# A two-layer transformer kernel on one core: scalings and copies moved to ScalarE, five element-wise steps to GpSimd, tanh products in pairs, and a new order of the work

## The chip, the core and the metric

The program runs on one core of a Trainium2 chip. The core's engines run their own instruction queues side by side: TensorE (PE; its weight loads are listed as PEld), VectorE (DVE), ScalarE (ACT), GpSimd (POOL) and SyncE (SP), which here only issues DMAs. An engine executes its queue strictly in order; between engines, work is ordered by semaphores. The metric is the device time of one execution in microseconds (us), the median of several runs.

## The reference, cut to what matters

Input: `hidden_states` of shape (8, 256, 128): 8 sequences of 256 tokens with 128 features, all in float32. Four blocks, each with a residual and a layer norm in front:

```python
x = x + L0_attn(layernorm(x))   # 16 heads of 8, softmax, relative positions (rel_k, rel_v, clipped at 20)
x = x + L0_ffn(layernorm(x))    # per token: softmax attention between its 16 heads, then 8 experts mixed by a softmax gate
x = x + L1_attn(layernorm(x))   # linear attention by a second-order Taylor expansion, 8 heads of 16
x = x + L1_ffn(layernorm(x))    # top-2 of 8 experts + a shared one: silu((x@w1+b1)*(x@w3+b3)) @ w2 + b2
```

The silu is computed with a tanh: `h * (1 + tanh(h))` on halved values.

## The kernel before

One sequence ("image" t, 0 to 7) is the unit. Its 256 tokens lie as 2 blocks (`C = 2`) of 128 partitions. The work of one image is cut into 141 small *pieces* (`norm0`, `scores` 0 to 7, `turn` 0 to 15, `dot` 0 to 3, `chunk` 0 to 14, `join` 0 to 4 and so on), in five lists: PREPARE (first layer norm, q/k/v), ATTENTION (the softmax attention), FEED (attention between heads, gate, experts), SECOND (Taylor attention), LATE (routing, hidden chunks, expert sum, store).

**The order.** Each piece has a position, a whole number written by hand in `PREPARE_AT`, `ATTENTION_AT`, `FEED_AT`, `SECOND_AT` and `LATE_AT` (L83 to L108). Piece k of image t stands at `t * PERIOD + position`, with `PERIOD = 480`. Every engine walks through all pieces sorted by this number (`turns`, L329) and issues what it has to do in each. So four to five images are in work at a time: beside the attention of image t each engine does the FEED of t-1, the SECOND of t-2 and the LATE of t-2 and t-3. The 8 `scores` pieces stand at 0, 60, 120 ... 420. In this text *slot k* is the stretch of positions from 60k up to 60(k+1), taken modulo 480; each slot begins with the piece `scores` k. No position is a time: it only fixes the order in the queues.

**What the pieces that matter do.**
- `scores` k: 32 matmuls on PE (L1026, L1036) into two PSUM banks, a maximum on DVE (L725), an exponential on ACT (L451). PE may start `scores` k+1 only when the exponential of k is done. `turn` transposes the weights (L1047; evicted by ACT, L459), `relative` multiplies them with the table of relative values (L1065, L1068). After the last ones `keep_rv` 3 (ACT, L435) lets SP write `rvs` to DRAM (L373, 8 DMAs) and read it back as `relo` (L376, L378); `divide` (DVE, L731 to L739) needs it.
- `moments` (DVE, L678): a layer norm's mean and variance: 2 `bn_stats` and 6 small instructions that combine the halves. `normed` (DVE, L695): the scaling, one instruction a block. GpSimd takes the -0.5th power (L544, L579, L595, L606).
- `dot`, `dot_sum`, `soft`, `soft_sum`, `mix`, `mix_sum`, `mix_scale` (FEED, nearly all DVE, L768 to L813): the attention between heads of a token: 4 products and 4 sums of 1024 elements a partition, a softmax over 512 elements, again 4 products and 4 sums.
- `chunk` n (LATE): two matmuls of 256 columns (L1224, L1225), an addition on ACT (L516), a product on DVE (L934: u), tanh on ACT (L521), and a second product on DVE (L939: hidden). 13 chunks an image. All but the last two images use one PSUM bank for them, the last two use two.
- `join` n: the experts' output matmuls (L1245 to L1254), added up by DVE (L947, L953) in the same bank, so `join` n+1 on PE waits for the DVE part of `join` n.
- `rank` (DVE, L904 to L927): the top-2 choice, twelve small steps one after another. `divide3` (DVE, L872 to L886), `qkv3` with the copy of v (DVE, L870), `scale2` (DVE, L825), `split0` (DVE, L712) whose result goes out by DMA and comes back as `qc` for GpSimd's `blocks` (L545 to L559), which `scores` 0 and 4 need.

## Time and profile before

| | |
|---|---|
| median of 3 runs | 813.42 us (812.59 to 817.56) |
| the profiled execution | 821.41 us, its span 819.6 us |
| busy in the span | PE 671.8, PEld 532.3, DVE 567.0, ACT 393.2, POOL 153.0 us |
| mean granted TensorE clock | 0.937 (1.00 from about 265 to 683 us) |

The span runs from the first to the last instruction. Each engine's busy time is the sum of its instructions' spans with overlaps counted once. The TensorE clock is given as a share of full speed. The profile names the instruction by engine, line and operands; "x8" is a count of instructions; a float32 matmul or transpose shows as one or two instructions, depending on the operation. "Idle before, releaser" is the engine's idle time ahead of an instruction and what ended it.

### The profile page before, as it was taken

Reading aid. Unit: us, or ns where it says so; the run is one execution under the profiler, and the core shown is the slowest. Engines: PE = TensorE matmul, PEld = TensorE weight load, DVE = VectorE, ACT = ScalarE, POOL = GpSimd, SP = SyncE. Lnnn points to the kernel's source line nnn. Section 1 sums busy time; section 2 is a strip of 40 time slices with the busy share of each in tenths; the row PEclk is TensorE's granted clock in tenths of the full one; section 3 lists DMA queues with packets and bytes.
Section 4 is the critical chain, followed back from the end, with each engine's and each line's share of the span. In section 5 each row is a group of like instructions: output and inputs, shape, how many; then the busy total and the mean of one; then the engine's idle time right before and its main releaser. Section 6 shows DMA issues by size and latency. Waiting matters only on the chain.

```text
span 819.6 us, 16984 instructions
## 1 busy us (share of the span) xinstructions
PE 671.8 (82%) x6432; PEld 532.3 (65%) x6432; DVE 567.0 (69%) x1482; ACT 393.2 (48%) x953; POOL 153.0 (19%) x179
## 2 busy tenths in 40 slices
PE   2377772887799899989998999889998995877886
PEld 1256651775587678767886688668876773656655
DVE  3122178458876997699769985998589857787174
ACT  1164333544565556555556555665565453324241
POOL 2311120412040205030403041202221102011000
...
DMA packets 75958, 13.45 MB, mean 16 GB/s; under 512 B 69851, under 2 KB 74981, under 8 KB 75749
## 3 DMA queue, kind: packets, MB, share of 16 engines
...
q0 software_dynamic: 384, 1.05, 0.4%
q10 hardware_dynamic: 180, 0.48, 0.2%
...
## 4 chain that ended last, share of the span: by engine, by line
PE 39%; issue 34%; DVE 12%; ACT 6%; POOL 3%; SPq 3%; DMA 2%; POOLq 0%; ACTq 0%
PE bank L1026 5%; PE bank L1047 4%; PE bank L1224 4%; PE bank L1065 3%; PE bank L1225 3%; PE bank L1145 3%; DVE nmx L725 2%; PE bank L1089 2%; PE bank L1036 2%; ACT pm L451 2%; POOL q3h L602 2%; PE bank L1178 1%; SPq L373 1%; SPq L349 1%; PE bank L965 1%
## 5 line engine op out<-in xcount | busy, mean ns | idle before, releaser
L451 ACT ACTIVATE pm<-bank,nmx 128x256 f32<-128x256 f32 x256 | 100.5, 475 | 126.3 <-DVE nmx L725 126.3
L725 DVE TENSOR_REDUCE nmx<-bank 128x2 f32<-128x512 f32 x128 | 82.3, 684 | 72.7 <-PE bank L1036 72.6
L1047 PE MATMUL bank<-w,pm 128*128 128x128 f32 x512 | 84.5, 291 | 29.6 <-ACT pT L459 24.4
L1026 PE MATMUL bank<-kT,qbd 64*64 64x256 f32 x1024 | 90.7, 417 | 13.2 <-issue 12.9
L459 ACT ACTIVATE pT<-bank 128x512 f32<-128x512 f32 x128 | 77.2, 603 | 38.1 <-PE bank L1047 37.9
L1047 PEld LDWEIGHTS bank<-w,pm 128*128 128x128 f32 x512 | 63.7, 151 | 42.7 <-ACT pm L451 30.5
L934 DVE SCALAR_TENSOR_TENSOR hu<-bank,w,ha 128x256 f32<-128x256 f32 x104 | 50.1, 482 | 53.3 <-ACT ha L516 52.9
L1065 PE MATMUL bank<-tv,pT 128*128 128x128 f32 (+1 forms) x512 | 84.7, 284 | 0.0
L1065 PEld LDWEIGHTS bank<-tv,pT 128*128 128x128 f32 x512 | 75.0, 202 | 3.5 <-issue 2.1
L516 ACT ACTIVATE ha<-bank,w 128x256 f32<-128x256 f32 x104 | 49.7, 478 | 55.1 <-PE bank L1225 54.2
L1224 PE MATMUL bank<-xfT,w 128*128 128x256 f32 x208 | 66.6, 402 | 8.5 <-DVE hu L934 8.5
L1225 PE MATMUL bank<-xfT,w 128*128 128x256 f32 x208 | 62.5, 382 | 0.0
L1036 PE MATMUL bank<-tkw,qr 64*64 64x96 f32 (+1 forms) x1024 | 56.4, 269 | 0.0
L1036 PEld LDWEIGHTS bank<-tkw,qr 64*64 64x64 f32 x1024 | 47.5, 143 | 13.5 <-issue 2.5
L501 ACT ACTIVATE sq<-bank,half_root 128x512 f32<-128x512 f32 x64 | 40.9, 698 | 29.7 <-PE bank L1178 29.7
L1178 PE MATMUL bank<-q3h,k 64*128 64x256 f32 x256 | 40.1, 434 | 13.5 <-ACT sq L501 10.7
L1026 PEld LDWEIGHTS bank<-kT,qbd 64*64 64x64 f32 x1024 | 33.4, 142 | 25.8 <-issue 23.2
L521 ACT ACTIVATE ht<-hu 128x256 f32<-128x256 f32 x104 | 43.1, 414 | 7.0 <-DVE hu L939 6.3
L939 DVE SCALAR_TENSOR_TENSOR hu<-ht,hu 128x256 f32<-128x256 f32 x104 | 45.9, 448 | 0.4 <-ACT ht L521 0.4
L557 POOL TENSOR_TENSOR qr<-qc,half_mask 128x512 f32<-128x512 f32 x32 | 33.5, 1068 | 67.3 <-DMA qc<-d_qdh 67.3
L606 POOL TENSOR_TENSOR rs_c<-ve_c,expo 128x2 f32<-128x2 f32 x8 | 5.6, 700 | 211.7 <-DVE ve_c L693 211.7
L853 DVE SCALAR_TENSOR_TENSOR x<-bank,gl,x 128x128 f32<-128x128 f32 x128 | 35.9, 343 | 12.6 <-PE bank L1145 12.5
...
## 6 DMA issues: line engine op xcount, KB each, us to landing
...
```

Of the source, the lines that this page charges most:

```text
L451: a = act.activation(pm[:, s % 2, c, j], b_s[c][:, j * S:(j + 1) * S], exp, bias=nmx[:, i:i + 1])
L459: act.activation(view(pT, (c * RTC + 2 * s) * C * P, [[1, 2 * C * P]]), b_t[:], copy).then_inc(pT_ready[0], 1)
L516: act.activation(ha[:, n % 2], late_bank(t, n)[:, 0:S], idn, scale=0.5, bias=wc("b1", n, n + 1)).then_inc(a_ready[0], 1)
L725: v.tensor_reduce(nmx[:, i:i + 2], b_s[c][:].rearrange("p (j k) -> p j k", j=2), AX_X, ALU.max, negate=True).then_inc(max_ready[0], 1)
L934: v.scalar_tensor_tensor(hu[:, n], late_bank(t, n)[:, S:2 * S], wc("b3", n, n + 1), ha[:, n % 2], ALU.add, ALU.mult).then_inc(u_ready[0], 1)
L1026: mm(b_s[c][cols:cols + P // 2, j * S:(j + 1) * S], qbd[rows:rows + P // 2, i], kT[rows:rows + P // 2, t % 2, u], start=True, stop=False, ...
L1036: a = mm(b_s[c][cols:cols + P // 2, j * S + lo:j * S + hi], qr[rows:rows + P // 2, i], tkw[rows:rows + P // 2, KB // QI - 1 - i % (KB // Q ...
L1047: a = nc.tensor.transpose(b_t[:, (j * 2 + kc) * P:(j * 2 + kc + 1) * P], chunk(pm[:, s % 2, c, j], kc), ident)
L1065: a = mm(b_rv[:, at:at + n], pT[:, i, c], tv[:, v0 * D0:v0 * D0 + n], start=True, stop=not corner)
L1178: a = mm((b_b, b_a)[half][:, kc * S:(kc + 1) * S], chunk(k3[rows:rows + P // 2], kc), q3h[rows:rows + P // 2, n], start=True, stop=True, t ...
L1224: mm(bk[:, 0:S], wc("W1", n * P, n * P + P), xfT[:], start=True, stop=True)
L1225: mm(bk[:, S:2 * S], wc("W3", n * P, n * P + P), xfT[:], start=True, stop=True).then_inc(ab_ps[0], 1)
```

## The change

Sizes and results stay; who does a step, and when, changes.

- **DVE to ACT:** the scaling `xn` (`scale0`) and `xl` (`scale1`), as `rs * x + nb` with `nb = -mean * rs`; the scaling `h2` (`scale2`); the copies of v (`qkv3` on DVE, now in `sum3` on ACT).
- **DVE to POOL:** the subtraction of the softmax maximum (`soft`), the product with the reciprocal sum (`mix_scale`), the product with the reciprocal denominator (`divide3`), and two steps of `rank`. POOL also computes `nb` (two small products each in `norm0` and `root1`).
- **DVE:** `moments` combines with `bn_aggr` (2 instructions) in place of 5 small ones. The tanh and the hidden product take two chunks at a time (7 of each an image, 13 before).
- `x1` has two buffers; `lsum` shares `lmx`, `y` shares `xl`.
- All five lists of positions are new. The depth from `norm0` to `store` goes from 2080 to 2160 positions; `PERIOD` stays 480.

```diff
-PREPARE_AT = [-337, -315, -287, -256, -179, -62, 15]
+PREPARE_AT = [-348, -315, -271, -212, -112, 24, 32]
-ATTENTION_AT = [0, 60, 120, 180, 240, 300, 360, 420, 41, 65, 93, 109, 168, 184, 194, 254, 257, 281, 347, 358, 406, 428, 438,
-                454, 70, 129, 155, 184, 202, 232, 258, 273, 319, 345, 375, 395, 429, 444, 463, 466, 188, 296, 404, 468, 213,
-                74, 485, 501, 528, 543, 537, 548, 553, 579]
+ATTENTION_AT = [0, 60, 120, 180, 240, 300, 360, 420, 86, 115, 133, 140, 163, 194, 231, 263, 264, 270, 358, 376, 392, 408,
+                442, 463, 121, 125, 146, 202, 254, 255, 259, 275, 317, 330, 384, 392, 430, 458, 471, 471, 220, 291, 402, 476,
+                37, 73, 496, 516, 526, 551, 531, 554, 567, 590]
-FEED_AT = [589, 609, 611, 639, 652, 660, 663, 667, 670, 674, 680, 682, 685, 690, 690, 695, 701, 704, 714, 723, 723, 733,
-           734, 736, 736, 749, 761, 767, 768, 827, 852, 877, 905, 926, 973, 1005]
+FEED_AT = [595, 603, 609, 612, 617, 623, 627, 659, 667, 671, 674, 686, 701, 705, 719, 723, 730, 730, 735, 736, 739, 752,
+           758, 765, 773, 796, 817, 826, 829, 883, 901, 917, 927, 953, 964, 983]
-SECOND_AT = [1031, 1044, 1076, 1147, 1153, 1164, 1169, 1175, 1176, 1196, 1206, 1214, 1215, 1215, 1215, 1218, 1218, 1224,
-             1246, 1252]
+SECOND_AT = [997, 1005, 1053, 1087, 1109, 1150, 1161, 1173, 1188, 1205, 1223, 1238, 1251, 1262, 1277, 1290, 1303, 1314,
+             1322, 1328]
-LATE_AT = [1282, 1307, 1308, 1350, 1396, 1419, 1443, 1454, 1470, 1492, 1511, 1546, 1552, 1591, 1613, 1617, 1621, 1644,
-           1650, 1676, 1688, 1697, 1727, 1743]
+LATE_AT = [1348, 1358, 1364, 1398, 1426, 1438, 1444, 1469, 1479, 1518, 1532, 1563, 1572, 1577, 1635, 1643, 1668, 1674,
+           1690, 1709, 1726, 1758, 1807, 1812]
...
+            def normed(dst, src, rs, nb):                      # ScalarE
+                for c in range(C):
+                    a = act.activation(dst[:, c], src[:, c], idn, scale=rs[:, c:c + 1], bias=nb[:, c:c + 1])
+                return a
+                if name == "scale0":
+                    act.wait_ge(*raised(rstd_a, t, 3))
+                    act.wait_ge(*raised(xnT_ps, t, 0))
+                    normed(xn, xin, rs_a, nb_a).then_inc(xn_ready[0], 1)
+                elif name == "scale2":
+                    act.wait_ge(*raised(rstd_y, t, 1))
...
+                        a = act.activation(h2[:, c], y[:, c], copy, scale=rs_b[:, 0, c:c + 1])
...
-                    if 1 <= n <= NCH:
-                        act.wait_ge(*raised(u_ready, t, n))
-                        act.wait_ge(*raised(hid_ready, t, n - 2))
-                        act.activation(ht[:, (n - 1) % 2], hu[:, n - 1], ACT.Tanh).then_inc(tanh_ready[0], 1)
+                    if 2 <= n < NCH and n % 2 == 0 or n == NCH:
+                        k = (n - 1) // 2
+                        m = min(2, NCH - 2 * k)
+                        act.wait_ge(*raised(u_ready, t, 2 * k + m))
+                        act.wait_ge(*raised(hid_ready, t, k))
+                        act.activation(ht[:, 0:m], hu[:, 2 * k:2 * k + m], ACT.Tanh).then_inc(tanh_ready[0], 1)
...
+                elif name == "soft":                               # GpSimd
+                    pool.wait_ge(*raised(l_max, t, 1))
+                    g.tensor_tensor(view(lg, 0, [[H0, C * H0], [1, H0]]), view(lg, 0, [[H0, C * H0], [1, H0]]),
+                                    view(lmx, 0, [[1, C * H0], [0, H0]]), ALU.subtract).then_inc(l_sub[0], 1)
...
+                elif name == "rank":                               # GpSimd
+                    pool.wait_ge(*raised(sc_steps, t, 5))
+                    g.tensor_tensor(tied[:], tied[:], view(w, W_AT["earlier"][0], [[0, C], [NE, NE], [1, NE]]), ALU.mult).then_inc(sc_steps[0], 1)
+                    pool.wait_ge(*raised(sc_steps, t, 6))
+                    g.tensor_tensor(above[:], above[:], tied[:], ALU.add).then_inc(sc_steps[0], 1)
...
-                v.tensor_tensor(mv[:], st[:, :, 1:3], st[:, :, 4:6], ALU.add)
-                v.tensor_tensor(st[:, :, 0], st[:, :, 1], st[:, :, 4], ALU.subtract).then_inc(steps[0], 1)
+                for c in range(C):
+                    a = v.bn_aggr(mv[:, c], st[:, c])
+                a.then_inc(steps[0], 1)
                 dve.wait_ge(*raised(steps, t, 2))
...
+                return v.tensor_scalar(ve, mv[:, :, 1], LN_EPS, None, ALU.add)
...
-                    if n >= 2:
-                        dve.wait_ge(*raised(tanh_ready, t, n - 1))
-                        v.scalar_tensor_tensor(hu[:, n - 2], ht[:, n % 2], 1.0, hu[:, n - 2], ALU.add, ALU.mult).then_inc(hid_ready[0], 1)
+                    if n >= 3 and n % 2 == 1 or n == NCH + 1:
+                        k = (n - 2) // 2
+                        m = min(2, NCH - 2 * k)
+                        dve.wait_ge(*raised(tanh_ready, t, k + 1))
+                        v.scalar_tensor_tensor(hu[:, 2 * k:2 * k + m], ht[:, 0:m], 1.0, hu[:, 2 * k:2 * k + m],
+                                               ALU.add, ALU.mult).then_inc(hid_ready[0], 1)
```

## Rows read from the trace of the kernel before

**Rows 1.** Timeline, DVE: the sum x1 that ends an image's attention (4 of 8).
```profile
102.76 0.42 DVE L744 TENSOR_TENSOR x<-bank,xres 128x256 f32<-128x256 f32 x1 [2.85 <-PE bank L1003]
...
264.78 0.42 DVE L744 TENSOR_TENSOR x<-bank,xres 128x256 f32<-128x256 f32 x1
...
600.22 0.42 DVE L744 TENSOR_TENSOR x<-bank,xres 128x256 f32<-128x256 f32 x1
681.28 0.42 DVE L744 TENSOR_TENSOR x<-bank,xres 128x256 f32<-128x256 f32 x1
```

**Rows 2.** Windows: one period cut at the maxima of `scores`, slots 2 to 7, 0, 1.
```profile
352.74:360.25 7.51, 6.94 (x65) 5.38 (x66) 6.73 (x23) 4.63 (x12) 1.56 (x3) 1.00 0.01 2
360.25:380.40 20.15, 17.54 (x148) 13.35 (x149) 19.31 (x28) 12.26 (x30) 2.73 (x2) 1.00 0.00 1
380.40:396.47 16.07, 14.19 (x131) 11.40 (x132) 14.76 (x41) 7.30 (x18) 2.01 (x3) 1.00 0.01 2
396.47:402.30 5.83, 5.83 (x68) 5.14 (x68) 4.83 (x17) 3.67 (x9) 2.94 (x4) 1.00 0.29 55
402.30:406.54 4.24, 4.24 (x53) 3.60 (x54) 2.95 (x10) 3.32 (x9) 1.23 (x2) 1.00 0.36 21
406.54:415.50 8.96, 8.96 (x83) 7.76 (x84) 5.93 (x15) 5.30 (x12) 4.97 (x5) 1.00 0.01 2
415.50:427.46 11.96, 11.83 (x192) 9.48 (x192) 7.01 (x20) 6.26 (x15) 0.00 (x0) 1.00 0.21 24
427.46:436.76 9.30, 8.11 (x73) 6.51 (x74) 8.16 (x34) 5.81 (x15) 3.39 (x5) 1.00 0.06 17
sum 84.02, PE 77.64 PEld 62.62 DVE 69.69 ACT 48.55 POOL 18.82; mean PE 9.70 PEld 7.83 DVE 8.71 ACT 6.07 POOL 2.35
```

Columns of these rows: stretch, its length, then busy us (and instructions) of PE, PEld, DVE, ACT, POOL, then granted clock, DMA share, GB/s.

**Rows 3.** Timeline, PE: joins back to back, at full clock.
```profile
809.89 0.60 PE L1252 MATMUL bank<-w,hu 128*128 128x256 f32 x2
...
811.64 0.60 PE L1252 MATMUL bank<-w,hu 128*128 128x256 f32 x2
```

**Rows 4.** Groups by form, whole run, DVE: moved or paired operations (busy us, mean ns).
```profile
L939 DVE SCALAR_TENSOR_TENSOR hu<-ht,hu 128x256 f32<-128x256 f32 x104 | 45.9, 448 | 0.4 <-ACT ht L521 0.4
L787 DVE TENSOR_TENSOR lg<-lg,lmx 128x512 f32<-128x512 f32 x8 | 5.5, 692 | 0.3
L885 DVE TENSOR_TENSOR o<-o,den 128x256 f32<-128x256 f32 x8 | 3.4, 424 | 0.3
L920 DVE TENSOR_TENSOR tied<-tied,w 128x128 f32<-128x128 f32 x8 | 2.3, 292 | 0.3
```

**Rows 5.** Timeline, DVE: one `moments`, and a scaling of two blocks.
```profile
355.38 0.47 DVE L681 BATCH_NORM_STATS2 st_a<-xin 128x6 f32<-128x128 f32 x2
...
356.63 0.17 DVE L693 TENSOR_SCALAR ve_a<-mv_a 128x2 f32<-128x2 f32 x1
...
357.62 0.60 DVE L697 TENSOR_SCALAR xn<-xin,mv_a,rs_a 128x128 f32<-128x128 f32 x2
```

**Rows 6.** Groups by form, whole run, POOL and ACT: the nearest operations of the new places.
```profile
L557 POOL TENSOR_TENSOR qr<-qc,half_mask 128x512 f32<-128x512 f32 x32 | 33.5, 1068 | 67.3 <-DMA qc<-d_qdh 67.3
...
L569 POOL TENSOR_TENSOR v<-vraw,r 128x128 f32<-128x128 f32 x16 | 8.3, 541 | 0.0
...
L478 ACT ACTIVATE hh<-y 128x128 f32<-128x128 f32 x16 | 5.0, 310 | 10.2 <-DVE y L817 9.9
```

**Rows 7.** Timeline: a hidden product of DVE while POOL works.
```profile
409.41 2.10 POOL L557 TENSOR_TENSOR qr<-qc,half_mask 128x512 f32<-128x512 f32 x2
...
410.44 1.35 DVE L939 SCALAR_TENSOR_TENSOR hu<-ht,hu 128x256 f32<-128x256 f32 x1
```

**Rows 8.** Timeline: from the last eviction of `rvs` to its use.
```profile
414.03 0.60 ACT L435 ACTIVATE rvs<-bank 128x512 f32<-128x512 f32 x1 [0.50 <-PE bank L1065]
...
421.83 1.39 SPq L378 DMA_DIRECT2D relo<-d_rv  x2
...
427.15 0.25 DVE L731 RECIPROCAL rden<-bank 128x16 f32<-128x16 f32 x1
```

More of the change, by code:

```diff
@@ L111 @@
 ALL_AT = PREPARE_AT + ATTENTION_AT + FEED_AT + SECOND_AT + LATE_AT
+DRIFT = 0
+STEP = [PERIOD + (DRIFT if k >= len(PREPARE + ATTENTION) else 0) for k in range(len(ALL))]
 PIECES = sorted([(at, k, piece) for k, (piece, at) in enumerate(zip(ALL, ALL_AT))])
+TURNS = [(t, piece) for _, _, _, t, piece in sorted([(t * STEP[k] + at, at, k, t, piece) for at, k, piece in PIECES for t in range(B)])]
 assert len(ALL_AT) == len(ALL)
-FIRST, LAST = PIECES[0][0], PIECES[-1][0] + (B - 1) * PERIOD
 W_COLS = [("ident", P), ("head_mask", H0), ("query_mask", QI), ("head_mask3", H1), ("earlier", NE * NE), ("half", P),
@@ L329, in turns @@
         def turns(piece):
-            for at in range(FIRST, LAST + 1):
-                for pos, _, (name, n) in PIECES:
-                    t, off = divmod(at - pos, PERIOD)
-                    if off == 0 and 0 <= t < B:
-                        piece(t, name, n)
+            for t, (name, n) in TURNS:
+                piece(t, name, n)
         @block.sync
@@ L492, in rest @@
                 elif name == "sum3":
+                    act.wait_ge(*raised(v3_ps, t, 1))
+                    for c in range(C):
+                        a = act.activation(view(v17, c * V17, [[D1 + 1, H1], [1, D1]]), view(b_b, c * E, [[D1, H1], [1, D1]]), copy)
+                    a.then_inc(v3_ready[0], 1)
                     act.wait_ge(*raised(vsum_ps, t, 1))
@@ L591, in rest @@
                     pool.wait_ge(*raised(x3_ready, t - 1, 0))
-                    g.tensor_tensor(x2[:, t % 2], x1[:], y[:], ALU.add).then_inc(x1_sum[0], 1)
+                    g.tensor_tensor(x2[:, t % 2], x1[:, t % 2], y[:], ALU.add).then_inc(x1_sum[0], 1)
                 elif name == "norm3":
@@ L684, in moments @@
                 dve.wait_ge(*raised(steps, t, 1))
-                v.tensor_tensor(mv[:], st[:, :, 1:3], st[:, :, 4:6], ALU.add)
-                v.tensor_tensor(st[:, :, 0], st[:, :, 1], st[:, :, 4], ALU.subtract).then_inc(steps[0], 1)
+                for c in range(C):
+                    a = v.bn_aggr(mv[:, c], st[:, c])
+                a.then_inc(steps[0], 1)
                 dve.wait_ge(*raised(steps, t, 2))
-                v.tensor_scalar(mv[:, :, 0], mv[:, :, 0], 0.5, None, ALU.mult)
-                v.scalar_tensor_tensor(st[:, :, 3], st[:, :, 0], E / 4, st[:, :, 0], ALU.mult, ALU.mult).then_inc(steps[0], 1)
-                dve.wait_ge(*raised(steps, t, 3))
-                v.tensor_tensor(mv[:, :, 1], mv[:, :, 1], st[:, :, 3], ALU.add).then_inc(steps[0], 1)
-                dve.wait_ge(*raised(steps, t, 4))
-                return v.tensor_scalar(ve, mv[:, :, 1], 1 / E, LN_EPS, ALU.mult, ALU.add)
+                return v.tensor_scalar(ve, mv[:, :, 1], LN_EPS, None, ALU.add)
             def normed(dst, src, mv, rs):
@@ L742, in piece @@
                     dve.wait_ge(*raised(xres_ready, t, 1))
-                    dve.wait_ge(*raised(x1_sum, t, 0))
-                    v.tensor_tensor(x1[:], b_o[:, 0:C * E].rearrange("p (c e) -> p c e", c=C), xres[:], ALU.add).then_inc(x1_ready[0], 1)
+                    dve.wait_ge(*raised(x1_sum, t - 1, 0))
+                    v.tensor_tensor(x1[:, t % 2], b_o[:, 0:C * E].rearrange("p (c e) -> p c e", c=C), xres[:], ALU.add).then_inc(x1_ready[0], 1)
                 else:
@@ L820, in rest @@
                     v.tensor_scalar(ve_b[:, 0], ss[:], 1.0 / E, RMS_EPS, ALU.mult, ALU.add).then_inc(ss_eps[0], 1)
-                elif name == "scale2":
-                    dve.wait_ge(*raised(rstd_y, t, 1))
-                    dve.wait_ge(*raised(h2T_ps, t, 0))
-                    for c in range(C):
-                        a = v.tensor_scalar(h2[:, c], y[:, c], rs_b[:, 0, c:c + 1], None, ALU.mult)
-                    a.then_inc(h2_ready[0], 1)
                 elif name == "gate":
@@ L866, in rest @@
                     normed(h3, x2[:, t % 2], mv_c, rs_c).then_inc(h3_ready[0], 1)
-                elif name == "qkv3":
-                    dve.wait_ge(*raised(v3_ps, t, 1))
-                    for c in range(C):
-                        a = v.tensor_copy(view(v17, c * V17, [[D1 + 1, H1], [1, D1]]), view(b_b, c * E, [[D1, H1], [1, D1]]))
-                    a.then_inc(v3_ready[0], 1)
                 elif name == "divide3":
@@ L918, in rest @@
                     v.tensor_tensor(tied[:], others, mine, ALU.is_equal).then_inc(sc_steps[0], 1)
-                    dve.wait_ge(*raised(sc_steps, t, 5))
-                    v.tensor_tensor(tied[:], tied[:], view(w, W_AT["earlier"][0], [[0, C], [NE, NE], [1, NE]]), ALU.mult).then_inc(sc_steps[0], 1)
-                    dve.wait_ge(*raised(sc_steps, t, 6))
-                    v.tensor_tensor(above[:], above[:], tied[:], ALU.add).then_inc(sc_steps[0], 1)
                     dve.wait_ge(*raised(sc_steps, t, 7))
```

86 lines of the change are left out of this document (49 added, 37 removed).

## The prediction

> **What bounds the kernel now.** I read three views. First the page: PE is the busiest engine (82% of the span), DVE next (69%), and the chain that ended last is spread over all engines, so no single share names the bound. Then the timeline of the sum x1, which DVE makes once an image [rows 1]. It cuts the span into: 102.8 us up to the first; two intervals of together 162.0 (264.78 - 102.76); four of together 335.4, so 83.9 each; one of 81.1; and a tail of 819.6 - 681.3 = 138.3 us. Third, one of the steady periods cut at the eight `scores` pieces [rows 2]. This view decides. In the stretches of slots 3 and 4 (20.15 and 16.07 us) DVE is busy 19.31 and 14.76 us and PE only 17.54 and 14.19; DVE's few gaps there are the 0.03 to 0.3 us between dependent steps. In slots 5, 6, 7 and 0 (5.83, 4.24, 8.96, 11.96) PE is busy all the time and DVE 4.83, 2.95, 5.93, 7.01. Slots 2 and 1 are mixed. So the period is not bound by one engine. It is DVE first and PE next, because the order puts nearly all products of the head attention into two slots. PE is busy 77.64 of 84.02 us, DVE 69.69.
>
> That gives a rule that can be tested on the old order: a slot takes what its slower engine needs. For PE I count columns of the pieces in a slot: 811.64 - 809.89 = 1.75 us for a join of 4 x 256 columns, thus 0.44 us for 256 [rows 3]; matmuls in different quarters of the array go side by side. This gives 11.2, 7.1, 6.0, 15.2, 12.8, 5.2, 3.7, 8.6 us for slots 0 to 7. For DVE I add the steps from start to start: 7.2, 8.8, 7.0, 20.2, 15.7, 5.6, 3.1, 5.2. In slots 0, 5, 6, 7 the measured 31.0 us stand against 28.7 of PE (factor 1.08), in slots 1 to 4 the measured 53.0 against 51.7 of DVE (1.025) [rows 2]. With these factors the rule gives 84.0 for the old period; it is fitted to the sum, but it also gives each slot within 0.6 us.
>
> **The change part by part, for one image.** DVE loses: in `moments`, 356.63 + 0.17 - 355.38 = 1.42 us [rows 5]. The two `bn_stats` (0.47) and the last step stay. Two `bn_aggr` have no row; between one small step (0.17) and a `bn_stats` each, I take 0.25 for both, and 1.0 for the whole: 4 x 0.42 = 1.7. `xn`, `xl`, `h2` and the copies of v: 0.60 for two blocks [rows 5], with 0.5 for the last two, together 2.1. (The last two read one operand less, hence the 0.5, an estimate; 0.60 is the upper bound.) Softmax subtraction 0.69, `mix_scale` and `divide3` 0.42 each [rows 4]. Hidden products in pairs: 256 elements more cost 692 - 424 = 268 ns, so about 156 ns of a 424 ns instruction are fixed, most of which a pair saves once: 6 x 0.13 = 0.8 [rows 4]. The two steps of `rank`: 0.58 [rows 4], but nothing stands behind them in DVE's queue, for its next step reads their result. POOL needs 0.54 for each [rows 6] and two more hops, so DVE idles about 1.2 us in place of 0.6 of work; this item is a loss of 0.6. Net about 5.5 us, DVE's need falls from 72.7 to 67.2.
>
> ACT gets 8 instructions of about 0.31 us or a little more (there is no row with both a scale and a bias from a tile) [rows 6], about 2.3 us, and gives back 1.0 by the paired tanh. At 48.55 busy of 84.02 [rows 2] it hides this, except where it waits in order: in `scale2` it stands idle for DVE's and POOL's root (a small DVE step of 0.17 [rows 5], a POOL step that I take below the 1.07 of rows 6 at 0.7, and hops: 1.2 us) with the eviction of `turn` 10 behind it. POOL gets 1.07 for the subtraction, about 0.74 each for the two products (between 0.54 for 128 and 1.07 for 512 elements), 1.08 for `rank` and four tiny ones, bounded by 0 and 0.54, taken as 0.35: 5.1 us on top of 18.82 busy [rows 2, 6]. It is hidden by POOL's idle time; what reaches the path are the hops. The softmax chain grows from 0.69 to 1.07 plus a hop, but DVE has the next `scores` maxima (1.3 us) to do meanwhile; after `mix_scale` there are 23 positions to `turn_mix`.
>
> The new order moves more than the handovers do. By the same sums the new slots 0 to 7 need on PE 9.9, 5.3, 10.8, 7.2, 13.5, 6.2, 7.6, 9.1, and on DVE 7.7, 5.0, 9.2, 10.8, 14.6, 5.3, 7.9, 6.8 (the wait in `rank` counted). Two dots and `up` now stand in slot 2, under the PE work of `qkv3`, `down`, `up` and chunks; `divide3`, `join` 3 and 4, `out1`, `scale4` went from slot 4 to 5 and 6. With the factors the larger need of each slot is 10.7, 5.7, 11.7, 11.1, 15.0, 6.7, 8.2, 9.8: 78.9 us. On top: in slot 4 `join` 1 on PE ends about 1 us after DVE wants it, and ACT's wait in `scale2` lies in a thin slot; part of both is covered, I add 0.9. **Period 79.8 us** in place of 83.9.
>
> Moved waits: `keep_rv` 3 to `divide` 0 shrinks from 69 to 55 positions. The way through DRAM started at 414.03, its last copies were issued at 421.83 for 1.39 us, and DVE used them at 427.15 [rows 8]; so they landed between 423.2 and 427.15, 9 to 13 us after the start, and I take 11. In the new order PE needs 9.9 x 1.08 = 10.7 us for slot 0 ahead of the use, so it is about level; up to 1 us would fall on DVE, which has 3 us to spare there. `split0` goes from 301 to 368, ahead of `scores` 0 of the next image at 480: 14 to 15 us of queue. It needs two DMA steps one after another, as the chain of rows 8 has, so at most that chain's 11 us, and 2.1 us of POOL behind it [rows 7]. On POOL `qkv3` now stands ahead of `norm0`, so the first norm waits behind its two products; `turn0` is 77 positions later and covers it. Two buffers for `x1` and the shared tiles change no wait that shows in the profile.
>
> **The sum.** Start up to the first x1: 103, for it has no FEED work and hangs on tables and on `scores` one after another. The two early intervals: DVE's dots between `scores` 3 and 5 are their longest part, and the tail of the softmax chain (`out1`, `scale2`) no longer stands ahead of `scores` 5: 162.0 - 8 = 154. Four at 79.8: 319.2. The last: 81.1 - 3.6 = 77.5. The tail has no attention to cover hops: less DVE work in the head attention (-3), more hops in `rank`, `divide3` and the softmax (+1.7): 137. Sum 790.7 us, 28.9 less than the span of 819.6. The profiled execution of before took 821.41 us, 1.8 more than its span, and the median of the runs is 8.0 below it: 790.7 + 1.8 - 8.0 = 784.5, **785 us**.
>
> **Rivals.** (B) The new handovers put waits into the thin slots, as each queue is in order; the period then ends between the two, at 82, and the other parts gain half: 4 x 1.9 + 6 = 13 to 14 us, about 800. For it: the rule is fitted to one order. Against it: the new order leaves 10 to 70 positions between nearly all producers and users on other engines. (C) The slots come out at 77 because dense work leaves PE no pipeline starts, and the early intervals gain more: 4 x 6.9 + 18, about 768. (D) DVE and POOL hinder each other: while POOL ran its 2.10 us, the hidden product on DVE took 1.35 us [rows 7], against a mean of 0.448 over all 104 [rows 4]. If all of the added 5.1 us of POOL work fell on DVE steps of this sort in slots that DVE bounds, the period would be 84.9, above 83.9; from 4.1 us of it on, nothing is left of the gain. That would give about 825 with a longer tail. Against it: the subtraction and `mix_scale` run beside the maxima of `scores`, the products of `divide3` beside `join` 3, and neither of these kinds ever shows a longer time beside POOL. In the Trainium skill, SBUF - State Buffer, section "Who interferes with whom", the port pair that DVE and GpSimd share is an exclusive lock, taken by DVE instructions with two inputs in SBUF; by that rule the trace agrees (1.35 against 0.448 us), and the outcome would be this rival only where such instructions meet.
>
> **How the numbers follow.** Forecast (777 to 793) 0.60, B 0.20, C 0.10, D or a smaller gain that ends within 1% or above 0.10. About 1% is what can be told from no change here. The range leaves out the end of C and all beyond B: 772 to 802. Faster by over 1% (below 805) 0.88, within 1% 0.07, slower 0.05.
>
> **What would show it.** Right: four equal intervals of x1 near 80 us, PE idle under 3 us a period, DVE busy about 63 to 64, and slots 3 and 4 together near 26 us in place of 36. Wrong in a step: DVE idle over 1 us ahead of the reduction in `rank` or the softmax sum; ACT idle ahead of `h2` with PE waiting behind; DVE waiting for `relo` at `divide` 0; hidden products far above 0.66 us. A tail above 140 us would mean that the hops weigh more than the work.

## The result, and the profile after

The changed kernel takes 773.6 us (median; 772.77 to 775.27) against 815.05 us for the kernel before in runs on the same chip: the ratio is 0.949, with an interval of 0.946 to 0.953. The forecast was 785 with a range of 772 to 802, so the result lies 1.6 us above the lower end of the range and below the 777 to 793 that was given the highest chance. The profiled execution of the new kernel has a span of 771.8 us.

The first view is the timeline of DVE, the sum x1 (five of the eight images; start, duration, instruction, then the idle time before it).

```profile
94.69 0.42 DVE L794 TENSOR_TENSOR x<-bank,xres 128x256 f32<-128x256 f32 x1 [2.48 <-PE bank L1027]
...
164.42 0.43 DVE L794 TENSOR_TENSOR x<-bank,xres 128x256 f32<-128x256 f32 x1 [1.80 <-PE bank L1027]
...
239.34 0.41 DVE L794 TENSOR_TENSOR x<-bank,xres 128x256 f32<-128x256 f32 x1
...
560.80 0.41 DVE L794 TENSOR_TENSOR x<-bank,xres 128x256 f32<-128x256 f32 x1
...
638.70 0.41 DVE L794 TENSOR_TENSOR x<-bank,xres 128x256 f32<-128x256 f32 x1
```

The same cuts as in [rows 1] give, before and after (us): start 102.8 and 94.7; two early intervals 162.0 and 144.65; four steady ones 335.4 and 321.5 (80.4 each); the last 81.1 and 77.9; the tail 138.3 and 133.1. A steady interval gains 3.5 us, an early one 8.7.

The page's first part (busy us, share of the span, instructions) has PE at 84% where it was 82%, and DVE at 67% where it was 69:

```profile
PE 647.4 (84%) x6432; PEld 518.4 (67%) x6432; DVE 517.3 (67%) x1234; ACT 403.6 (52%) x969; POOL 176.8 (23%) x252
```

The second view answers to [rows 2]: windows over one steady period, cut at the maxima of `scores`, slots 2 to 7, 0 and 1 (busy us of PE, PEld, DVE, ACT, POOL, then granted clock, DMA share, GB/s).

```profile
321.53:335.06 13.53, 12.29 (x100) 9.99 (x102) 9.45 (x20) 8.70 (x22) 5.54 (x11) 1.00 0.04 12
335.06:345.07 10.01, 8.24 (x92) 5.66 (x90) 9.98 (x13) 7.67 (x17) 0.00 (x0) 1.00 0.01 2
345.07:359.64 14.57, 14.57 (x137) 11.88 (x134) 13.86 (x24) 9.23 (x22) 1.69 (x2) 1.00 0.00 1
359.64:366.19 6.55, 6.52 (x72) 5.68 (x71) 5.05 (x19) 3.39 (x12) 1.53 (x3) 1.00 0.00 1
366.19:374.53 8.34, 8.34 (x86) 7.50 (x86) 6.08 (x21) 5.88 (x15) 3.22 (x6) 1.00 0.22 40
374.53:384.23 9.70, 9.70 (x87) 8.53 (x87) 6.45 (x22) 5.19 (x12) 7.91 (x8) 1.00 0.21 14
384.23:394.76 10.53, 10.49 (x184) 8.39 (x184) 7.46 (x26) 5.42 (x12) 0.72 (x1) 1.00 0.20 24
394.76:401.75 6.99, 6.12 (x61) 4.89 (x62) 5.08 (x16) 4.45 (x11) 1.09 (x2) 1.00 0.01 2
sum 80.22, PE 76.27 PEld 62.51 DVE 63.41 ACT 49.92 POOL 21.70; mean PE 9.53 PEld 7.81 DVE 7.93 ACT 6.24 POOL 2.71
```

Slots 3 and 4 were 36.2 us and are 24.6. Slot 4, in which DVE was busy 14.76 of 16.07 us before [rows 2], is now full on PE (14.57 of 14.57). Slot 2 went the other way, from 7.5 to 13.5 us, and is the one slot in which both engines stand idle for over 1 us (PE 1.24, DVE 4.08).

### The profile page after: what moved, and what is told of

It is laid out like the page before. It is cut to its first block and busy times, and to the rows that moved or that the text cites. A ratio compares the mean times of both kernels' runs of the same rounds, so it can differ in the third digit from the quotient of the medians.

```text
span 771.8 us, 16793 instructions
## 1 busy us (share of the span) xinstructions
PE 647.4 (84%) x6432; PEld 518.4 (67%) x6432; DVE 517.3 (67%) x1234; ACT 403.6 (52%) x969; POOL 176.8 (23%) x252
## 5 line engine op out<-in xcount | busy, mean ns | idle before, releaser
L1050 PE MATMUL bank<-kT,qbd 64*64 64x256 f32 x1024 | 88.3, 408 | 15.2 <-issue 12.8
L1071 PE MATMUL bank<-w,pm 128*128 128x128 f32 x512 | 80.1, 280 | 17.7 <-ACT pT L471 16.5
L1089 PE MATMUL bank<-tv,pT 128*128 128x128 f32 (+1 forms) x512 | 80.5, 281 | 1.2 <-ACT rvs L447 1.2
L1071 PEld LDWEIGHTS bank<-w,pm 128*128 128x128 f32 x512 | 60.1, 144 | 31.0 <-ACT pm L463 17.7
L1089 PEld LDWEIGHTS bank<-tv,pT 128*128 128x128 f32 x512 | 72.0, 198 | 7.8 <-issue 5.0
L1248 PE MATMUL bank<-xfT,w 128*128 128x256 f32 x208 | 67.0, 404 | 8.9 <-DVE hu L955 8.8
L1249 PE MATMUL bank<-xfT,w 128*128 128x256 f32 x208 | 63.7, 389 | 0.0
L1202 PE MATMUL bank<-q3h,k 64*128 64x256 f32 x256 | 38.1, 416 | 13.1 <-ACT sq L527 10.7
L1248 PEld LDWEIGHTS bank<-xfT,w 128*128 128x128 f32 x208 | 34.6, 196 | 18.5 <-DVE hu L955 14.7
L1249 PEld LDWEIGHTS bank<-xfT,w 128*128 128x128 f32 x208 | 40.7, 196 | 5.9
L977 DVE SCALAR_TENSOR_TENSOR xo<-bank,rw,xo 128x128 f32<-128x128 f32 x128 | 36.0, 344 | 12.9 <-PE bank L1278 12.4
L1276 PE MATMUL bank<-w,hu 128*128 128x256 f32 x128 | 40.3, 397 | 1.3 <-DVE xo L977 1.3
```

The costliest lines, as they stand in the source:

```text
L1050: mm(b_s[c][cols:cols + P // 2, j * S:(j + 1) * S], qbd[rows:rows + P // 2, i], kT[rows:rows + P // 2, t % 2, u], start=True, stop=False, ...
L1071: a = nc.tensor.transpose(b_t[:, (j * 2 + kc) * P:(j * 2 + kc + 1) * P], chunk(pm[:, s % 2, c, j], kc), ident)
L1089: a = mm(b_rv[:, at:at + n], pT[:, i, c], tv[:, v0 * D0:v0 * D0 + n], start=True, stop=not corner)
L1202: a = mm((b_b, b_a)[half][:, kc * S:(kc + 1) * S], chunk(k3[rows:rows + P // 2], kc), q3h[rows:rows + P // 2, n], start=True, stop=True, t ...
L1248: mm(bk[:, 0:S], wc("W1", n * P, n * P + P), xfT[:], start=True, stop=True)
L1249: mm(bk[:, S:2 * S], wc("W3", n * P, n * P + P), xfT[:], start=True, stop=True).then_inc(ab_ps[0], 1)
```

## The experiments

Twelve kernels ran beside before and after. All were read in the same way; the period is the mean of the four steady intervals of x1, "early two" is the sum of the two before them, and slot 2 is that of the four steady periods (lowest and highest where they differ by over 0.3 us). Ratios are to the kernel before, on the same chip.

| kernel | median us | ratio (interval) | early two | period | slot 2 | tail |
|---|---|---|---|---|---|---|
| before | 815.05 | 1 | 162.0 | 83.9 | 7.5 | 138.3 |
| after | 773.6 | 0.949 (0.946 to 0.953) | 144.7 | 80.4 | 13.5 | 133.1 |
| e1, all but the order | 823.4 | 1.011 (1.002 to 1.021) | 157.9 | 85.4 | 8.7 | 137.9 |
| e2, order alone | 833.7 | 1.022 (1.015 to 1.029) | 160.9 | 88.2 | 17.2 to 17.9 | 137.2 |
| e3, `rank` back | 784.0 | 0.960 (0.953 to 0.968) | 145.6 | 81.3 | 13.5 | 137.9 |
| e4, no pairs | 775.2 | 0.950 (0.946 to 0.955) | 145.0 | 80.4 | 13.1 | 131.3 |
| e5, first image | 814.7 | 1.000 (0.995 to 1.004) | 161.6 | 83.8 | 7.5 | 138.9 |
| f1, ScalarE's four back | 815.4 | 1.001 (0.998 to 1.004) | 154.9 | 85.5 | 17.8 | 138.5 |
| f2, GpSimd's three back | 779.2 | 0.957 (0.952 to 0.962) | 146.9 | 80.7 | 13.5 | 133.2 |
| f3, old `moments` | 785.0 | 0.965 (0.959 to 0.970) | 144.2 | 81.9 | 14.2 | 135.9 |
| f4, xl and v back | 804.7 | 0.986 (0.981 to 0.991) | 147.6 | 84.1 | 15.7 to 18.3 | 136.2 |
| f5, xl back | 791.9 | 0.970 (0.965 to 0.976) | 144.0 | 83.5 | 15.2 to 18.1 | 136.4 |
| c1, hh earlier | 769.9 | 0.947 (0.941 to 0.952) | 145.1 | 79.7 | 12.8 | 133.2 |
| c2, c1 and three moves | 787.1 | 0.967 (0.961 to 0.973) | 147.9 | 81.8 | 12.8 | 134.7 |

### The two halves: e1 and e2

e1 is the new kernel with the five old lists of positions (so the handovers, `bn_aggr` and the pairs without the order), e2 the old kernel with the new lists. The first list of e1:

```diff
-PREPARE_AT = [-348, -315, -271, -212, -112, 24, 32]
+PREPARE_AT = [-337, -315, -287, -256, -179, -62, 15]
...
```

> The changed kernel with the five position lists of the kernel before: the handovers, bn_aggr and pairs alone. Slot rule: the old order keeps both heavy slots, DVE needs 19.0 and 14.1 us there, the larger needs of the slots add up to 79.7 us, and with the 1.3 us by which the rule fell short in the changed kernel the period is about 81; start and early intervals lose little (first x1 at 102 to 103), so 798 to 804 us. Rival 'the handovers carry the gain': period near 80.2, first x1 near 95, 775 to 785 us. Rival 'hops eat the work': 812 us or more.

> The kernel before with the five new position lists and nothing else: DVE keeps all its work. Slot rule: 80.2 us plus about 1, period about 81.3; first x1 near 95 as in the changed kernel, early intervals together about 150, tail about 137: 780 to 788 us. Rival 'the order only pays with the lighter DVE': slots 3 and 4 stay DVE-bound at the old sum, period 83 or more, 800 us or more.

Neither half alone is faster: e2 is slower by 1.5 to 2.9%, e1 by 0.2 to 2.1%, just clear of no change. Together they gain 5%. The period is 83.9 without either, 85.4 and 88.2 with one, 80.4 with both. The rule of the prediction (a slot takes what its slower engine needs) had given 79.7 to 81 for e1 and 81.3 for e2, so it fails on both by 4 to 7 us. The timeline of DVE in e1, from the end of slot 2 to slot 4, shows why less work was not less time:

```profile
354.06 0.42 DVE L813 TENSOR_TENSOR q<-bank,r 128x256 f32<-128x256 f32 x1 [2.69 <-ACT dT L484]
...
361.12 1.81 DVE L824 TENSOR_TENSOR prod<-q,kv 128x1024 f32<-128x1024 f32 x1
...
364.10 1.23 DVE L824 TENSOR_TENSOR prod<-q,kv 128x1024 f32<-128x1024 f32 x1
...
370.13 0.69 DVE L837 TENSOR_REDUCE lmx<-lg 128x32 f32<-128x512 f32 x1 [1.12 <-ACT lg L487]
```

The subtraction that went to GpSimd (0.69 us) comes back as a wait of 1.12 us for the exponential; between the maximum and the sum of the softmax the old order has DVE do only two additions of 0.49 us together. (In after this wait is 0.64 us.) The product at 361.12 takes 1.81 us in place of 1.23 while GpSimd's product of q3h runs (358.88, 2.98 us). DVE stands idle for 2.69 us ahead of q at the end of slot 2. So slots 3 and 4 fall only from 36.2 to 35.2, and slot 2 rises from 7.5 to 8.7. In e2 slots 3 and 4 do fall (24.9), so the reason that the second expectation gave for its rival (both slots stay long) was wrong; there slot 2 takes 17 to 18 us, at a granted clock of 0.81 to 0.90.

### One part taken back at a time: f1, f2, f3, e3, e4

f1 puts `xn`, `xl`, `h2` and the copies of v back on DVE; f2 the subtraction, `mix_scale` and `divide3`; f3 has the old `moments`; e3 the two steps of `rank` on DVE; e4 a tanh and a product for each chunk. All keep the new order. The core of each:

```diff
# f1 (xl; the other three likewise)
+                    normed(xl, x1[:, t % 2], mv_b, rs_b[:, 0]).then_inc(xl_ready[0], 1)      # DVE
# f2 (divide3; the other two likewise)
-                elif name == "divide3":                                                      # GpSimd
-                    g.tensor_tensor(view(o3, ...), view(o17, ...), view(den3, ...), ALU.mult)
+                    v.tensor_tensor(view(o3, ...), view(o17, ...), view(den3, ...), ALU.mult) # DVE
# f3
-                    a = v.bn_aggr(mv[:, c], st[:, c])
+                (the old steps that combine the halves)
# e3
-                    g.tensor_tensor(tied[:], tied[:], ..., ALU.mult)                         # GpSimd
+                    v.tensor_tensor(tied[:], tied[:], ..., ALU.mult)                         # DVE
# e4
-                    if 2 <= n < NCH and n % 2 == 0 or n == NCH:
+                    if 1 <= n <= NCH:
```

> The changed kernel with ScalarE's four handovers (xn, xl, h2, the copies of v) back on DVE. Theory 'chain in slot 2': xl, the copies of v and xn again stand in DVE's queue around hh and ahead of the dots, in the slot that took 13.5 us with PE idle for 1.2; it grows by 2 to 3 us and PE's idle time may pull the granted clock down there as in the run of the new order alone. Period 82.5 to 84, 793 to 802 us. Rival 'only DVE's sum in DVE-bound slots counts' (slots 3 and 4, where none of the four stands): period 80.2 to 80.8, 774 to 779 us.

> The changed kernel with the softmax subtraction, mix_scale and divide3 back on DVE (rank stays on GpSimd). By the trace DVE waited 0.6 us for the exponential behind the subtraction and had idle time in slot 5, so of the 1.5 us of work at most 0.7 comes onto the path: period 80.2 to 80.9, 773 to 780 us. Rival 'DVE's work counts in full in slots 3 and 4': period 81.3 or more, 783 us or more. Rival 'the hops cost more than the work': below 772 us.

> The changed kernel with the five small steps in place of bn_aggr. Four times 0.42 us of DVE work; by the chain theory only norm1 and norm0, which stand ahead of hh and of the dots, reach the path: period 80.6 to 81.2, 777 to 782 us. Rival 'all of it is hidden, slots 2, 1, 6 and 0 are not bound by DVE': 772 to 775 us.

> The changed kernel with the two steps of rank back on DVE. If the 0.6 us loss that the prediction charged is on the path of every image: 4 to 5 us less than the changed kernel. If it lies in a slot where PE is never idle (slot 6 of the changed kernel: 8.34 us, PE busy 8.34): the steady period stays at 80.2 to 80.4 and only the tail gains, 0.5 to 1.5 us in all.

> The new kernel with tanh and hidden product one chunk at a time, as before (13 of each an image in place of 7). Theory of the prediction: the pairs save DVE 0.8 us and ScalarE 1.0 us a period, of which the slots that DVE bounds show only a part: period 80.6 to 81.0, median 775 to 780. Rival: the pairs bring nothing or a loss, because the steady slots are bound by PE and by chains: period within 0.2 us of 80.4, median 771 to 775.

Taking the part back costs a period +5.2 us (f1), +0.3 (f2), +1.5 (f3), +0.9 (e3) and 0.0 (e4). The sum is 7.9. Taking all of them back at once is e2, 7.9 longer than after. In the new order the parts thus add up about, and ScalarE's four carry two thirds of it. That the sums agree to 0.1 us is in part chance, for the granted clock in slot 2 differs: 1.00 in after, 0.90 in f1, 0.90 and 0.81 in e2. Against their expectations f2 came out within its range and e4 at its rival's (period within 0.2 us); f1 (815.4 against at most 802, period 85.5 against at most 84) and f3 (785.0 against at most 782, 81.9 against at most 81.2) cost more than the theory allowed; in e3 both branches failed.

**`rank` (e3).** The prediction had counted this move as a loss of 0.6 us a period; it is a gain of 0.9. It stands in slot 6, 8.3 us in after and 9.2 in e3. The timeline of DVE and POOL, first after, then e3:

```profile
371.51 0.17 DVE L935 TENSOR_TENSOR sc<-sc,ssum 128x16 f32<-128x16 f32 x1
...
373.53 0.28 DVE L945 TENSOR_REDUCE rank<-above 128x16 f32<-128x128 f32 x1 [1.10 <-POOL above L663]
...
372.52 0.45 POOL L661 TENSOR_TENSOR tied<-tied,w 128x128 f32<-128x128 f32 x1 [2.19 <-DVE tied L943]
...
374.14 2.09 POOL L584 TENSOR_TENSOR qbd<-qT,half_mask 128x512 f32<-128x512 f32 x2
```

```profile
457.19 1.66 DVE L930 TENSOR_TENSOR sc<-sc,ssum 128x16 f32<-128x16 f32 x1
...
460.27 0.28 DVE L944 TENSOR_REDUCE rank<-above 128x16 f32<-128x128 f32 x1
...
456.71 2.09 POOL L584 TENSOR_TENSOR qbd<-qT,half_mask 128x512 f32<-128x512 f32 x2
```

The wait in `rank` is there, 1.10 us, as forecast. But a small DVE step of the same piece, ahead of the reduction, takes 1.66 us in e3 (1.66 to 1.81 in four of the eight images) and 0.17 or 0.18 in after, in all eight. In e3 GpSimd has nothing of `rank` to do and runs the product of `blocks` at that moment. In after its queue stands still 2.19 us for `tied`, and the product comes behind. From the start of that small step to the end of the last step of `rank`, which follows the reduction, it is 3.58 us in e3 and 2.70 in after, a difference of 0.88, which is what slot 6 differs by. In the Trainium skill, SBUF - State Buffer, section "Who interferes with whom", a DVE instruction with two inputs in SBUF is shut out while a GpSimd instruction that was issued first reads SBUF; the trace agrees (1.66 against 0.17 us). So the mechanism of rival D acts here, and with the opposite sign: the move keeps GpSimd's long product away from the small step. The median of e3 is 10 us above that of after, more than four periods account for (3.7); 4.8 us of it lie in the tail, of which more below.

**Pairs (e4).** A hidden product of 512 elements takes 0.68 us, two single ones 0.88, and over the whole kernel DVE spends 45.1 us on them without pairs and 36.0 with. Yet the period is the same to 0.04 us. With pairs slot 2 is 0.4 longer and slots 0 and 1 together 0.5 shorter. The rival, that it brings nothing in a period, was right.

### What fills slot 2: f5, f4 and c1

f5 puts only `xl` back on DVE, f4 `xl` and the copies of v. c1 keeps the new kernel's places and issues DVE's scaling `hh` one piece earlier:

```diff
# c1
-                elif name == "scale1":
+                elif name == "root1":
                     dve.wait_ge(*raised(rstd_b, t, 2))
```

> The new kernel with only the scaling xl back on DVE. Theory chain, narrow form: xl alone (two instructions ahead of hh, 1.2 us while GpSimd's product holds the port) is what shifts the transposes behind hh; slot 2 above 15.5 and the period above 82.3, the median above 787. Rival: the copy of v, which waits 0.9 us for PE in DVE's queue with the combination behind it, is the larger part; then xl alone leaves slot 2 below 14.7 and the period below 81.5, the median 772 to 783.

> The new kernel with only two of ScalarE's four new steps back on DVE: the scaling xl (scale1) and the copies of v (qkv3). Both stand in the chain norm1, root, turn1, down, dots that fills slot 2. Theory chain: with all four back slot 2 takes 17.9 us in place of 13.5 and the period 85.6 in place of 80.4; if it is these two that stand ahead of hh and of the transposes, slot 2 is again near 17.5 and the period 84 to 85, the median 803 to 812. Rival sum: each of the four costs its own DVE time, so two of four (1.1 us of 2.1) give a period near 81.5 to 83, slot 2 near 14.5 to 15.5, the median 780 to 795.

> The changed kernel with DVE's part of scale1 (the scaling hh) moved up behind root1, ahead of chunk 9. In the changed kernel DVE stood idle for 1.41 us before chunk 9's product and then took 1.42 us for hh (0.6 without GpSimd beside it), which PE's turn1 waited for. If the norm chain sets slot 2, it ends 1.5 to 2.5 us sooner, hh takes 0.6 us, slot 2 goes from 13.5 to 12.3 to 12.9: period 79.3 to 79.8, 766 to 771 us. If PE's own queue ahead of turn1 sets it, nothing moves: 772 to 775 us.

`xl` alone, 0.6 us of DVE work, costs 3.1 us a period and 18 us of the median. The copies of v add 0.6 more, and `xn` with `h2` another 1.4 (f1 against f4). The timelines of slot 2, first after, then f5 (DVE, PE and POOL):

```profile
325.22 1.42 DVE L750 TENSOR_SCALAR hh<-x,mv_b,rs_b 128x128 f32<-128x128 f32 x2
...
326.69 0.44 PE L989 MATMUL bank<-w,hh 128*128 128x128 f32 x2 [0.49 <-DVE hh L750]
326.96 0.60 PE L1248 MATMUL bank<-xfT,w 128*128 128x256 f32 x2
327.40 0.59 PE L1249 MATMUL bank<-xfT,w 128*128 128x256 f32 x2
...
325.51 2.04 POOL L649 TENSOR_TENSOR q3h<-q,half_mask 128x512 f32<-128x512 f32 x2 [2.10 <-ACT k L513]
```

```profile
330.49 1.42 DVE L746 TENSOR_SCALAR xl<-x,mv_b,rs_b 128x128 f32<-128x128 f32 x2
331.83 1.76 DVE L746 TENSOR_SCALAR hh<-x,mv_b,rs_b 128x128 f32<-128x128 f32 x2
...
333.64 0.69 PE L987 MATMUL bank<-w,hh 128*128 128x128 f32 x2 [2.17 <-DVE hh L746]
334.12 1.06 PE L1246 MATMUL bank<-xfT,w 128*128 128x256 f32 x2
334.98 1.06 PE L1247 MATMUL bank<-xfT,w 128*128 128x256 f32 x2
...
330.79 2.04 POOL L645 TENSOR_TENSOR q3h<-q,half_mask 128x512 f32<-128x512 f32 x2 [2.11 <-ACT k L509]
```

Three things follow one another. First, `xl` stands ahead of `hh` in DVE's queue. Second, both run beside GpSimd's product of q3h, and take 1.42 and 1.76 us for two blocks in place of 0.60 [rows 5]. Third, PE waits 2.17 us for `hh` in place of 0.49, and after that its matmuls take 1.06 us in place of 0.60. The windows of f5 for three of its four steady slots 2 show the third as a granted clock:

```profile
326.80:344.89 18.09, 15.17 (x100) 11.98 (x102) 11.06 (x21) 7.93 (x20) 5.57 (x11) 0.81 0.03 8
411.57:428.31 16.74, 13.82 (x100) 11.04 (x102) 11.06 (x21) 7.93 (x20) 5.57 (x11) 0.90 0.03 8
495.27:510.48 15.21, 12.29 (x100) 9.99 (x102) 11.06 (x22) 7.93 (x20) 5.57 (x11) 1.00 0.04 10
```

The same 100 matmuls keep PE busy 15.17 us at 0.81, 13.82 at 0.90, and 12.29 at 1.00, here as in after. Starts of neighbours are 0.86 us apart at 334.12 and 0.44 at 326.96: the two levels, 1.2 and 2.4 GHz. Of the 4.56 us between the first of these slots and slot 2 of after, 2.88 are more busy time and 1.68 more idle time of PE. The last of the three windows sets the two apart: PE waits the same 2.17 us there, but the clock stays at 1.00, and the slot takes 15.21 us, just 1.68 more than in after. So the chain costs 1.7 us in every period, and the clock comes on top in three of the four (1.6, 2.9 and 1.5 us). In these three it fell behind the idle of 2.17 us; it did not fall behind the idles of 0.75 and 0.49 us in after. f4 shows the same: an idle of 2.66 us in each, and slots of 17.27, 15.70, 17.27 and 18.25 us at 0.90, 1.00, 0.90 and 0.81. A long wait of PE is thus no sure cause; what decides whether the clock falls behind it stays open.

c1 is the same chain turned the other way. Its DVE timeline has `hh` ahead of q3h:

```profile
324.57 0.60 DVE L750 TENSOR_SCALAR hh<-x,mv_b,rs_b 128x128 f32<-128x128 f32 x2 [0.36 <-POOL rs_b L614]
325.62 0.48 DVE L955 SCALAR_TENSOR_TENSOR hu<-bank,w,ha 128x256 f32<-128x256 f32 x1 [0.44 <-ACT ha L542]
```

`hh` takes 0.60 in place of 1.42, PE does not wait for it, slot 2 is 12.8 us, and in the period that was cut the other seven slots are as in after to 0.01 us. The period is 79.7 and the median 769.9, the lowest of all. Against after (0.947 with 0.941 to 0.952, 0.949 with 0.946 to 0.953) the intervals overlap, and the two were timed at different times, so a shorter time is not shown; what speaks for a gain is the period of the trace (79.7 against 80.4).

### Further moves of positions, and the first image: c2 and e5

```diff
# c2 (c1, and)
-                442, 463, 121, 125, 146, 202, 254, 255, 259, ...
+                442, 463, 121, 125, 146, 202, 235, 238, 259, ...
-LATE_AT = [1348, 1358, 1364, 1398, 1426, 1438, 1444, 1469, 1479, 1518, ...
+LATE_AT = [1348, 1358, 1364, 1398, 1426, 1438, 1444, 1469, 1501, 1518, ...
```

> The variant with hh right behind the root (slot 2 at 12.8 us, period 79.7) and two further moves of positions: the pieces relative 4 and 5 from 254 and 255 to 235 and 238, into slot 3, and one hidden chunk from slot 4 (position 1479) to slot 5 (1501). Slot 4 is bound by PE throughout (14.57 of 14.57 us busy). Theory: the PE work leaves slot 4 and slots 3 and 5 take it partly in gaps: period 79.0 to 79.5, median 764 to 769. Rival: PE is busy there too (8.24 of 10.0 and 6.5 of 6.5 us), and the work only changes its slot: period 79.6 to 80.0, median 769 to 772.

The expectation names the slots of the chunk wrongly: 1479 is 39 modulo 480, slot 0, and 1501 is 61, slot 1. The two `relative` pieces took 0.43 us out of slot 4 (14.57 to 14.14) and put 0.41 into slot 3: the rival, nothing gained. The chunk took 0.12 us out of slot 0 and put 2.2 into slot 1, which is 9.19 in place of 6.98: all that the period is longer than c1's. Neither range of the expectation (764 to 769 us, and 769 to 772 for the rival) holds; the median is 787.1. It is not PE's work, of which slot 1 has only 6.98 us in 9.19. The timeline of c2 (PE, then DVE) shows the wait:

```profile
401.09 0.70 PE L1248 MATMUL bank<-xfT,w 128*128 128x256 f32 x2
...
404.43 0.70 PE L1248 MATMUL bank<-xfT,w 128*128 128x256 f32 x2 [1.78 <-DVE hu L955]
...
406.64 0.70 PE L1248 MATMUL bank<-xfT,w 128*128 128x256 f32 x2 [0.43 <-DVE hu L955]
...
403.89 0.48 DVE L955 SCALAR_TENSOR_TENSOR hu<-bank,w,ha 128x256 f32<-128x256 f32 x1 [1.40 <-ACT ha L542]
```

Slot 1 now holds three chunks. They share one PSUM bank, so each has to go through ACT and DVE before PE may begin the next, which takes 3.34 and 2.21 us from start to start. With two chunks slot 1 hides this in its other work, with three it does not.

e5 is the old kernel in which only image 0 has its first pieces at the new positions:

```diff
+FIRST_AT = [-348, -315, -271, -212, -112, 24, 32] + ...      # used for t == 0 alone
```

> The kernel before; for image 0 alone the pieces of PREPARE, scores, turn, relative and keep_rv take their new positions, all else keeps the old order. If the 8 us by which the first x1 comes sooner are due to the first image's own order (each scores ahead of the transposes of the one before): first x1 at 94 to 97 us, all later intervals as before, 805 to 809 us. Rival 'it is the lighter DVE or the norm's chain': first x1 stays at 101 to 103, 813 to 816 us.

The median does not change (0.995 to 1.004). Its first x1 stands at 98.4 us, neither at the 94 to 97 of the one theory nor at the 101 to 103 of the other, and in every other experiment, with old or new order, at 95.5 to 97.8. The 102.8 of the profiled execution of before and the 94.7 of after lie on both sides of these. The traces show what sets them apart. From 60 to 94 us PE was granted 0.85 of its clock in before, 0.95 in e5 and 0.97 in after, and up to the first x1 its matmuls kept it busy 59.3 us in before and 55.8 in e5, for nearly the same work (647 and 646 instructions). So of the 4.3 us between these two up to 3.5 are PE's busy time at a lower clock.

## Why the prediction came out as it did

**The sum.** Its total of 790.7 us stands against a span of 771.8. By its terms (forecast, measured): start 103, 94.7; early two 154, 144.65; four periods 319.2, 321.5; last 77.5, 77.9; tail 137, 133.1. The start's 8.3 us are for the most part no gain of the change: before's own profiled start was 4 to 7 us later than in all twelve experiments, old order and new. The prediction had taken 8.0 us off for the difference between profile and median, and after's profile and median do not differ (773.58 and 773.6). That two numbers of about 8 us cancel is luck; without it the forecast would have been 792.5. What is left of the error, 11 us of median, is the early intervals (9.4) and the tail (3.9), less 2.7 elsewhere. The direction and the steady period were right; the gain of the median, 41 us, was forecast as 28.

**The steady slots** were forecast at 11.7, 11.1, 15.0, 6.7, 8.2, 9.8, 10.7, 5.7 (slots 2 to 7, 0, 1) and came at 13.5, 10.0, 14.6, 6.6, 8.3, 9.7, 10.5, 7.0. So where the gain comes from was right: slots 3 and 4 together 24.6 us (26 forecast), DVE busy 63.4 us a period (63 to 64 forecast), PE idle 4.0 (under 3 forecast). Slot 4 has the right length for another reason: forecast as DVE's (15.0 for a need of 14.6), it is PE's, which is busy 14.57 of 14.57 us, DVE 13.86. Two slots were too low. Slot 2 lacks 1.8 us, because it is a chain over four engines (scaling, transposes, down, q, products) and not a sum of one engine's work. Slot 1 lacks 1.3: PE is busy for 6.12 of its 6.99 us and waits 0.68 of the rest for DVE's step of a chunk, the same round through one bank that c2 made longer. Slots 3 and 4 came 1.5 us shorter than forecast, and the 0.9 us added for two waits were not seen as such, so that the period is off by only 0.6 us is in part because errors cancel.

**The rule behind it** is what failed. It was fitted to one order. For the final kernel it gives 78.9 us, 1.5 too little, and 79.8 with the 0.9 us added by hand; for e1 and e2, made of the same parts, it is 4 and 7 us too little. It leaves out waits inside a queue, longer steps beside GpSimd, and the lower clock after a wait of PE. The final kernel has few of these and each half alone has many. Rival B's mechanism, handovers that put waits into queues that run in order, acts in e1 (1.12 and 2.69 us of DVE) and not, at that size, in the kernel that it was forecast for. In e2 nothing is handed over; there PE waits 2.66 us in slot 2 for `hh`, which stands behind the copies of v and `xl` in DVE's own queue.

**The early intervals.** The prediction gave each of them the gain of a steady one, 4 us; they gained 8.7. The windows cut the same way show the second of them at 11.2, 10.4, 11.4 us for slots 2, 3, 4 after and 8.1, 18.5, 17.6 before. Without the work of `LATE` slot 2 rises by only 3.0 us, not 6.0, and slot 4 is not yet held by PE at 14.6. So these three slots together fall by 11.1 us, in a steady period by 5.6 (43.7 to 38.1). A part of it is again the clock: before's slot 4 ran at 0.63 here and after's at 1.00 (PE busy 13.57 us for 95 instructions, 9.59 for 100), and over both early intervals the clock is 0.85 and 0.93, PE busy 123.8 and 119.1 us for as many matmuls. Which wait lets the clock fall there is not shown. Rival C had this term nearly right (18 us for the early intervals, 17.4 measured) and the period wrong (77, 80.4).

**The tail** gained 5.2 us, not 1.3. It is 131 to 133 us in e4, f2 and c1, 134.7 in c2, about 136 in f3, f4 and f5, and 137 to 139 in f1, e1, e2, e3 and e5. The windows from the last x1 to the end, before and after:

```profile
681.28:819.60 138.32, 106.54 (x544) 78.41 (x542) 86.71 (x252) 44.96 (x108) 13.22 (x14) 0.86 0.01 4
638.70:771.80 133.10, 100.93 (x544) 75.69 (x544) 79.42 (x210) 43.89 (x103) 16.67 (x24) 0.92 0.01 4
```

The same 544 matmul instructions keep PE busy 5.6 us less, at a clock of 0.92 in place of 0.86. In e3 they take 106.2 us at 0.89, in e4 99.4 at 0.94, and the tails there are 137.9 and 131.3. What PE stands idle in the tail is nearly the same in all four (31.7 to 32.2 us). So the gain, and the difference between after, e3 and e4, is PE's busy time at another granted clock; the prediction's sum (less DVE work, more hops) has no such term. Which wait lets the clock fall stays open.

**The signs that were named.** DVE waits 1.10 us ahead of the reduction in `rank`, over the 1 us that was to mean a wrong step; but the forecast had itself charged 1.2 us there, so the sign could not tell. It waits 0.64 us for the softmax sum. ACT stands idle 1.0 us ahead of `h2`, and PE does not wait behind it (slot 5: 6.52 of 6.55 us busy). DVE waits for `relo` in the first two images only (3.80 and 0.49 us). Hidden products stay at 0.68, the tail below 140.

**The prices of operations.** Right: two `bn_aggr` 0.25 us (0.25 estimated), the subtraction on GpSimd 1.06 (1.07), the paired product 0.68 (0.66), waits of DVE in `rank` 1.10 (1.2). Off without weight: scaling pairs on ACT 0.87 (0.6 to 0.65), products of GpSimd 0.62 (0.74), its tiny steps 0.20 (0.35), steps of `rank` on GpSimd 0.45 (0.54). From the groups by form of after:

```profile
L743 DVE BATCH_NORM_AGGREGATE mv_c<-st_c 128x2 f32<-128x6 f32 x32 | 4.0, 166 | 0.5
...
L624 POOL TENSOR_TENSOR lg<-lg,lmx 128x512 f32<-128x512 f32 x8 | 8.5, 1058 | 123.7 <-DVE lmx L834 123.7
...
L654 POOL TENSOR_TENSOR o<-o,den 128x256 f32<-128x256 f32 x8 | 5.0, 622 | 36.4 <-DVE den L911 36.4
...
L661 POOL TENSOR_TENSOR tied<-tied,w 128x128 f32<-128x128 f32 x8 | 3.6, 447 | 19.1 <-DVE tied L943 19.1
...
L413 ACT ACTIVATE xl<-x,nb_b,rs_b 128x128 f32<-128x128 f32 x16 | 7.0, 492 | 0.2 <-POOL nb_b L616 0.2
```

**The weights of the parts** were wrong in four places. ScalarE's four were worth 2.1 us of DVE work and are worth 5.2 us of period (the clock included), GpSimd's three 1.5 and 0.3, the pairs 0.8 and 0.0, `rank` -0.6 and +0.9; only `moments` fits (1.7 and 1.5). The work that a step takes from DVE does not tell its worth here; for `xl`, `hh` and `rank` the traces show that what stands behind the step in its queue, or beside it on GpSimd, does.

**Rival D** was given too small a field. It named hidden products, which stay at 0.68 in pairs. The instructions that do meet GpSimd are the scalings `hh` in slot 2 (1.42 in place of 0.60) and the small step of `rank` in e3. The scaling of one tile from SBUF with two numbers a partition was not on the prediction's list, although the trace of before has it in each of the eight images, 1.00 or 1.01 us in place of 0.60 while GpSimd adds (DVE, then POOL):

```profile
354.46 1.01 DVE L697 TENSOR_SCALAR hh<-x,mv_b,rs_b 128x128 f32<-128x128 f32 x2
...
354.62 0.76 POOL L584 TENSOR_TENSOR xl<-xl,r 128x256 f32<-128x256 f32 x1 [1.79 <-DVE xl L697]
```
In the Trainium skill, SBUF - State Buffer, section "Who interferes with whom", such scalings and copies can take the shared port as well; the trace agrees (1.42 against 0.60 us).
